# Reciprocal on packed data, variance and response at other places, and one more VectorE tap in four halves

## The reference

```
hdn  = layernorm(mean(x) @ w_fc1.T);  dyn_w = hdn @ w_fc2.T      # a 5x5 kernel for each image and channel
out  = depthwise_conv5x5(x, dyn_w)
out  = layernorm over channels(out) * ln2_w + ln2_b              # per pixel: mean and variance over 64 channels
out  = gelu(out @ w_expand.T)                                    # 64 -> 256 channels
gx   = sqrt(sum over pixels(out^2));  nx = gx / (mean over channels(gx) + eps)
out  = gamma * out * nx + beta + out
out  = out @ w_shrink.T + x                                      # 256 -> 64 channels
```

## Time and profile before

| | us |
|---|---|
| median of three runs | 827.21 |
| profiled execution, time | 827.7 |
| profiled execution, span | 826.0 |
| PE busy | 776.0 (94%) |
| DVE (VectorE) busy | 624.6 (76%) |
| ACT (ScalarE) busy | 398.9 (48%) |
| POOL (GpSimd) busy | 450.2 (55%) |
| chain that ended last, by engine | DVE 17%, PE 11%, ACT 6%, issue 4% |
| mean granted clock of TensorE, as a share of full | 0.982 |

### The profile page before, as it was taken

The page is one execution under the profiler, slowest core; times in us unless marked ns, Lnnn a source line. Parts: engine busy times, 40 slices in busy tenths (PEclk is TensorE's granted clock), DMA queues, the critical chain, the costliest instruction groups (busy, mean ns, idle before and its releaser), DMA issues. The chain is left out here.

```text
span 826.0 us, 15628 instructions
## 1 busy us (share of the span) xinstructions
PE 776.0 (94%) x5399; PEld 635.3 (77%) x5399; DVE 624.6 (76%) x1143; ACT 398.9 (48%) x491; POOL 450.2 (55%) x450
## 2 busy tenths in 40 slices
PE   5999999999999999999999997978899999999886
PEld 5999998999998999999999996644445445454332
DVE  3666666666665666666888887999999999999965
ACT  5591002777774000000000003459989999999981
POOL 2333333333333333335888884988978887888610
PEclk9999999999999999999999996889999999999999
DMA  6670000000000000000000002022233334433234
GB/s 145 162 179 0 0 0 0 2 0 0 0 0 1 1 0 0 0 0 1 1 0 0 0 0 50 25 64 72 77 81 80 90 92 109 104 79 83 55 77 102
DMA packets 61571, 35.81 MB, mean 43 GB/s; under 512 B 41504, under 2 KB 59488, under 8 KB 61536
## 3 DMA queue, kind: packets, MB, share of 16 engines
q1 hardware_dynamic: 59424, 34.83, 17.8%
q10 hardware_dynamic: 2112, 0.52, 0.3%
HBM read 17.85 MB, written 9.37 MB: 33 GB/s over the span
## 5 line engine op out<-in xcount | busy, mean ns | idle before, releaser
L504 PE MATMUL psum<-line_hi,taps_hi 128*128 128x256 f32 x1270 | 203.0, 292 | 11.8 <-DVE taps_lo L400 8.5
L518 PE MATMUL psum<-line_lo,taps_hi 128*128 128x256 f32 x1270 | 202.5, 291 | 0.8 <-DVE line_lo L453 0.8
L512 PE MATMUL psum<-line_hi,taps_lo 128*128 128x256 f32 x1270 | 202.2, 291 | 0.0
L453 DVE SCALAR_TENSOR_TENSOR line_lo<-psum,rest 128x256 fp32r<-128x256 f32 x254 | 108.0, 425 | 123.9 <-POOL rest L285 114.9
L504 PEld LDWEIGHTS psum<-line_hi,taps_hi 128*128 128x128 f32 x1270 | 177.1, 192 | 13.0 <-issue 9.3
L518 PEld LDWEIGHTS psum<-line_lo,taps_hi 128*128 128x128 f32 x1270 | 176.4, 191 | 1.9 <-DVE line_lo L453 1.7
L512 PEld LDWEIGHTS psum<-line_hi,taps_lo 128*128 128x128 f32 x1270 | 176.9, 191 | 0.0
L285 POOL TENSOR_TENSOR rest<-x,line_hi 128x256 f32<-128x256 f32 x127 | 82.9, 652 | 168.6 <-DVE line_hi L444 168.6
L337 ACT ACTIVATE by_h<-x (+1 forms) x128 | 85.7, 669 | 106.6 <-DVE x L433 105.0
L285 POOL TENSOR_TENSOR rest<-by_h,line_hi 128x256 f32<-128x256 f32 x127 | 91.5, 720 | 83.3 <-DVE line_hi L444 83.3
L793 POOL TENSOR_TENSOR part<-part,prod 128x1008 f32<-128x1008 f32 (+2 forms) x56 | 127.5, 2276 | 17.1 <-ACT prod L860 11.3
(11 more groups left out here) (159 smaller groups left out, 760.6 us busy)
## 6 DMA issues: line engine op xcount, KB each, us to landing
stage<-in_x_dram SPq DMA_DIRECT2D x32, 256.0 KB, 4.0
rstd_wide<-rstd_dram SPq DMA_DIRECT2D x30, 256.0 KB, 5.3
out_dram<-x SPq DMA_DIRECT2D x28, 256.0 KB, 5.4
crossed<-x SPq DMA_DIRECT2D x16, 256.0 KB, 3.5
crossed<-x SPq DMA_DIRECT2D x16, 240.0 KB, 3.6
rstd_dram<-rstd SPq DMA_DIRECT2D x15, 64.0 KB, 1.5
out_dram<-x ACTq DMA_DIRECT2D x4, 128.0 KB, 4.7
out_dram<-x SPq DMA_DIRECT2D x4, 128.0 KB, 4.0
```

The costliest lines, as they stand in the source:

```text
L453: dve.scalar_tensor_tensor(out=line_lo[:, (slot + 1) % SLOTS, :, part], in0=as_lines(line_ps[slot][:, 0:LINE]), scalar=0.0, in1=as_lines(r ...
L504: mm = pe.matmul(line_ps[slot][:, 0:LINE], taps_hi[:, s, d, :], line_hi[:, slot, :, d:d + WP], start=(d == 0), stop=(d == OFFSETS - 1))
L512: pe.matmul(line_ps[slot][:, 0:LINE], taps_lo[:, s, d, :], line_hi[:, slot, :, d:d + WP], start=False, stop=False, skip_group_check=True)
L518: mm = pe.matmul(line_ps[slot][:, 0:LINE], taps_hi[:, s, d, :], line_lo[:, slot, :, d:d + WP], start=False, stop=(d == OFFSETS - 1), skip_ ...
```

## The change

- `EARLY` goes from halves 3, 4, 5, 6, 8, 10, 12, 14 to all of 3 to 14: halves 7, 9, 11 and 13 too have eleven VectorE taps and four products.
- The reciprocal of halves 0 to 14 works on packed data. SP copies the 16 partitions of `std` that hold data (four copies, each of 4x128 values) into `dense`, 128 partitions by 16 columns; VectorE waits for all four and takes the reciprocal of `dense`; the store to DRAM is 8 KB and not 64 KB. The spreading copies are of the same size as before.
- In slots without an energy sum `make_var` comes after three taps and not four. `make_rstd` comes after two more taps and after `finish(v,1)`; it was one tap after `make_var`.
- TensorE's `respond` comes ahead of `conv(3)` and not behind it.

```
-EARLY, EARLY_TAP = (3, 4, 5, 6, 8, 10, 12, 14,), ("up", 3)
+EARLY, EARLY_TAP = (3, 4, 5, 6, 7, 8, 9, 10, 11, 12, 13, 14,), ("up", 3)
...
+        PER = UCOLS // C
+        dense = sb("dense", [P, PER])
+        dense_rstd = sb("dense_rstd", [P, 2, PER])
...
-        rstd_dram = nc.dram_tensor("rstd_dram", [2, P, STAT_COLS], F32, kind="Internal").ap()
+        rstd_dram = nc.dram_tensor("rstd_dram", [2, P, PER], F32, kind="Internal").ap()
...
             def spread_rstd(u):
+                sp.wait_ge(std_ready, u + 1)
+                if u > 0:
+                    sp.wait_ge(rstd_ready, u)
+                for g in range(4):
+                    sp.dma_start(dense[32 * g:32 * g + 32, :],
+                                 std[32 * g:32 * g + 2 * SUBS, :].rearrange("q (a n) -> q a n", n=PER)).then_inc(std_dense, 16)
                 sp.wait_ge(rstd_ready, u + 1)
...
-                sp.dma_start(rstd_dram[u % 2], rstd[:, u % 2, :]).then_inc(rstd_stored[u % 2], 16)
+                sp.dma_start(rstd_dram[u % 2], dense_rstd[:, u % 2, :]).then_inc(rstd_stored[u % 2], 16)
...
-                rows = rstd_dram[u % 2].rearrange("(g q) n -> g (q n)", g=4)
+                rows = rstd_dram[u % 2].rearrange("(g h q) n -> g h (q n)", g=4, h=2)
...
-                    mine = rows[:, SUBS * h * STAT_COLS:SUBS * (h + 1) * STAT_COLS].rearrange("(a g) n -> a g n", a=1)
+                    mine = rows[:, h, :].rearrange("(a g) n -> a g n", a=1)
...
             def make_rstd(u):
-                dve.wait_ge(std_ready, u + 1)
                 if u > 1:
                     dve.wait_ge(rstd_stored[u % 2], 16 * (u // 2))
-                dve.reciprocal(rstd[:, u % 2, :], std[:, :]).then_inc(rstd_ready, 1)
+                if u < LAST:
+                    dve.wait_ge(std_dense, 64 * (u + 1))
+                    dve.reciprocal(dense_rstd[:, u % 2, :], dense[:, :]).then_inc(rstd_ready, 1)
+                else:
+                    dve.wait_ge(std_ready, u + 1)
+                    dve.reciprocal(rstd[:, u % 2, :], std[:, :]).then_inc(rstd_ready, 1)
...
                 take(2)
                 if v >= 0:
                     finish(v, 0)
-                take(2)
                 if n in range(UNITS) and n % 2 == 1:
+                    take(2)
                     sum_energy(n // 2)
+                else:
+                    take(1)
                 if w in range(UNITS):
                     make_var(w)
-                take(1)
+                take(2)
+                if v >= 0:
+                    finish(v, 1)
                 if w in range(UNITS):
                     make_rstd(w)
-                take(1)
-                if v >= 0:
-                    finish(v, 1)
                 take(1 + len(dve_taps(s)) - len(DVE_TAPS))
...
                 at_e(0, 1)
-                conv(3)
                 if n in range(UNITS) and n % 2 == 1:
                     respond(n // 2)
+                conv(3)
                 at_e(1, 0)
```

More of the change, by code:

```diff
@@ L655, in block_two @@
         rstd_spread = sem("rstd_spread")
+        std_dense = sem("std_dense")
         spread_made = sem("spread_made")
```

## The result

The changed kernel takes 846.94 us (median of four runs, 845.33 to 847.35) against 827.17 us: the ratio is 1.0233, 95% interval 1.022 to 1.0246, 19.8 us slower. Forecast was 829.2 us in a range of 823 to 837, so the size is far off. The profiled execution is the fastest of the four: 845.33 us with a span of 843.6 us, 17.6 us above the span of before.

What follows compares the result with a forecast made beforehand. VectorE's own order was taken as the bound. First four slots +2.79, halves 5 and 6 -0.21, four pairs -0.32, half 15 -0.24 gave +2.0 us; 827.7 + 2.0 - 0.5 = 829.2 us, range 823 to 837.

Steps and rivals of the forecast that it cites:

- The engine: Block two: VectorE, where the sum must be made, has no idle time to give; an 11/11 pair is 35.76 us.
- The taps and the response: Halves 7, 9, 11, 13 gain a tap; the earlier response removes a 0.8 us wait; pairs go from 35.63 to 35.76.
- The floor of 35.76: Pair of halves with 11 and 11 taps: pure VectorE work without a gap, 35.76 us.
- The packed reciprocal: VectorE, 15 halves before the last: 16 columns take 0.26 us, 0.27 between neighbours, saving about 0.60 us a half.
- The cover: VectorE work hiding the copies: ready at T+3.56 in odd halves, T+3.29 in even ones, T being the variance's start.
- L: Time from first issue of the four packed copies to the last landing, taken as 2.85 us; no change at 2.72.
- far ends: Outer bounds for the time from the copies' first issue to last landing: 2.2 and 5.3 us.
- near ones: Closer bounds for that time: 2.5 (0.33 a step) and 3.1 us (0.53 a step), both with a landing of 1.5.
- The first four slots: Slots 1 to 4, without finish: +1.02, +1.48, +0.41 and +0.68, less 0.80 for the response wait, sum +2.8 us.
- Costs taken as nothing: Later rstd (1.5 us in even halves, 0.3 in odd) hidden by GpSimd's wait for TensorE; SP's queue; the unchanged end.
- Rival 2: SP issues the copies slowly, 0.63 us a step: 8.3 us more, 837.4 us; chance 0.24.
- Rival 3: TensorE still sends the response late, held by ScalarE's gelu: 0.8 us waits stay in five pairs, +4, 833 us; chance 0.05.

Runs made afterwards that it cites:

- e10: Kernel before with eleven taps in all halves from 3 to 14 and nothing else of the change; 828.87 us, ratio 1.0008.
- e11: Kernel before with TensorE's response ahead of conv(3) and nothing else of the change; 823.85 us, ratio 0.9948.
- e3: Changed kernel with a single packed copy, not four, from half 1 on (output isn't the reference's); 826.47 us, ratio 0.9988.
- e4: Changed kernel with its reciprocal two taps later on VectorE, all four copies kept; 825.38 us, ratio 0.9971.
- e8: Changed kernel, packed reciprocal only from half 4 on and two taps later; halves 0 to 3 keep the old reciprocal and order; 822.87 us.
- e1: Changed kernel without packing: 128x128 reciprocal on std in its new place, copies left out, old store and spread; 832.30 us, ratio 1.0072.
- e9: As e8, but with ten taps in halves 7, 9, 11, 13 as in the kernel before; 821.28 us, ratio 0.9917.
- e6: Changed kernel with each copy writing 4 rows of 512 bytes, not 32 of 64, to a scratch tile; 842.05 us, ratio 1.0175.
- e7: Changed kernel with a half's statistics gathered in 16 neighbouring partitions, so that one copy of 128 rows packs them; 858.24 us, ratio 1.0359.
- e5: Changed kernel with two of the four packed copies issued by ScalarE behind its root, two by SP; 844.08 us, ratio 1.0195.

## Why the prediction was wrong

- **The engine.** Right. VectorE's own order is the bound in the pairs: 35.76 for 11/11 (e10), 0.9 us off when the wait for the response goes (e11), 34.6 without any wait (e3, e4, e8). In the first slots it is not VectorE alone (e3, e4).
- **The taps and the response.** The floor of 35.76 was right. What the prediction didn't say is that the two parts compete: the taps fill the time which the response's new place sets free. Each alone is harmless or a gain. Together, with the new places, a pair takes 36.03 us (e1); the two without the new places weren't run.
- **The packed reciprocal.** 0.25 us measured, 0.26 taken. What it costs in VectorE's order was 0.27 in the forecast and is 0.17: the next tap starts at 685.64, 0.17 us behind 685.47. So a half saves 0.69 and not 0.60 us. e1 and e3 agree: their pairs differ by 36.03 - 34.64 = 1.39 us, two reciprocals.
- **The cover.** T+3.56 and T+3.29 were forecast. In e3, where the reciprocal of these slots doesn't wait, it starts at 675.98 - 672.34 = T+3.64 in slot 9 and at 694.04 - 690.53 = T+3.51 in slot 10. The difference is the gap between neighbouring taps of e1, taken too small because the taps in the earlier trace rows had other work between them. It makes the cover longer and the work longer at once, so it doesn't help.
- **L: the step that failed.** "I take 2.85" should have been 4.06. Of the 1.2 us, 0.8 is the spacing of the issues (0.71 measured against 0.45) and 0.4 the landing (1.91 against 1.5), both from e3. The 0.45 a step lay between the lone store of 0.33 us and the small loads at the start, 0.53 on average; the landing was the store's. That store has no issue ahead of it, and it still holds SP for 0.32 us here. Nearer rows were in the trace and weren't used: `crossed`, the only copy within SBUF, holds SP for 0.51 and 0.60 us, and in block two SP issues two by two. SP in slot 9 of the kernel before, behind the store:

```profile
676.68 1.28 SPq L756 DMA_DIRECT2D rstd_wide<-rstd_dram  x2
678.01 1.35 SPq L742 DMA_DIRECT2D out_dram<-x  x2
```

That is 0.64 and 0.67 us an issue. With 0.67 a step and the landing of 1.5 the sum would have been 3.5 and 839 us, still short, since the landing too was too small. The measured L lies within the far ends of the prediction, 2.2 and 5.3; the range of 823 to 837 went with the near ones, and so it was too short. The Trainium skill's fixed cost of about 2.0 us (DMA: Bandwidth & Descriptors, "Anatomy of one DMA") agrees with the 1.91 us of one copy here, although it was read off another way of issuing. It was put aside because of the store.
- **The first four slots.** Forecast +2.8 us at L = 2.85, so 7.6 at 4.06. Measured at half 4: 599.43 - 594.37 = 5.1 us, and 5.8 when the earlier start of block two (528.80 against 529.52) is taken off. Slot 1 costs 1.4 and not 2.2 us: counted from the start of block two, the variance begins 0.7 us sooner than the forecast took (4.37 against 5.09 us). Slot 3 costs 0.9 and not 1.6: there 0.5 us of waits for TensorE and ScalarE are gone that the kernel before had. Slots 2 and 4 came within 0.4 and 0.1 us.
- **Costs taken as nothing.** GpSimd now waits for the factors (68.9 us in 13 waits) in place of TensorE, and no engine waits for GpSimd in the pairs: that cover held. It had help that the prediction didn't count: the copies that spread the packed factors land after 4.0 us and not 5.3 (medians); in e9, which has both forms, 5.3 for the halves with the old one and 4.1 for the packed ones. The end was not free: it loses 1.1 us. TensorE there, in the changed kernel:

```profile
805.79 3.59 PE L1327 MATMUL psum<-wide,shrink_now 128*64 128x512 f32 x8 [4.67 <-DVE x L1104]
```

and its stretch (the last columns are the granted clock, the DMA share and GB/s):

```profile
805.70:809.30 3.60, 3.50 (x8) 0.77 (x8) 1.24 (x3) 2.37 (x3) 1.95 (x1) 0.53 0.11 25
```

TensorE idles 4.67 us for VectorE, is then granted 0.53 of its clock, that is nearly all of the time 1.2 and not 2.4 GHz, and the eight matmuls take 3.59 us against 1.94 us in the kernel before, where the idle time ahead of them was 0.94 us. The last mean square is late by that: VectorE's wait for it is 3.8 us against 2.7. That the copies cause this isn't shown. e10, without any packing, loses the same (its wait is 3.9 us), and e1 idles 3.70 us at this place and then takes 1.94 us and waits 2.7. TensorE in e10:

```profile
789.29 3.63 PE L1312 MATMUL psum<-wide,shrink_now 128*64 128x512 f32 x8 [2.44 <-DVE x L1090]
```

Rival 2 of the prediction (slow issues, 837 us) came nearest, with the right place and too small a price. Rival 3 is out: the response's wait went.

In all, by the trace, in a pair (8 to 10): waits for the copies 1.41 + 1.52 = 2.93 us; two shorter reciprocals -1.38; the waits for the response and the shrink -0.81 and -0.18; the tap +1.3; the lost gaps +0.27. That sums to 2.1 us, and 2.12 was measured. Over the block: up to half 4 +5.06, halves 5 and 6 +1.97, four pairs +8.52, half 15 +0.95, the end +1.12, in all 17.62 us against 17.6 us between the two spans.

What stays open: why a packed copy holds SP for 0.7 us when the store of the factors takes 0.32, and why the landing is longer. That one side lies in DRAM isn't enough, for the stores of the output hold SP for 0.67 each. e6 only shows that the number of rows is the smaller part.

## What to carry to other kernels

A wait in an engine's own order costs its full length as soon as that engine is the bound, so a DMA that feeds such an engine must be priced at issues plus landing, with the spacing read from issues that stand one behind another in the same stretch and not from a lone one, before what it saves is counted. Count the instructions: four small copies cost four issues. When a trace shows that more work on an engine costs nothing, look for the wait that hides it, and take the wait away by itself first: here one moved line (e11) gave 4.3 us, and the packed reciprocal, once it was given enough cover and kept out of the first slots and without the four taps (e9), 2.6 us more.

## What the runs showed of the hardware

- A copy of 2 KB within SBUF takes 1.91 us from its issue to the instruction that waits for it, and the next issue on SP stands 0.71 us behind it (0.64 with rows of 512 bytes, e6). Alone it holds SP for 0.72 to 0.73 us (e3), one of 128 rows for 0.59 (e7), a store of 8 KB to DRAM for 0.32.
- 32 small matmuls (128x128, f32) that go to four groups of 32 columns take 1.1 us; the same to one group take 3.7 us (e7), both at a granted clock of 1.00.
- Two issues on ScalarE's queue keep ScalarE from its next instruction for 1.36 to 1.47 us in every slot but the first, where it is 2.0 (e5).
- A tap of VectorE that waits on a semaphore for the tap before it starts 1.28 us after it, an instruction without that wait 1.17 us after it. With `finish` and the reciprocal as neighbours, and so one such gap a slot unused, a pair takes 0.27 us more (e1 against e10).
- How long TensorE idles doesn't by itself tell the clock that it is granted next. The same eight shrink matmuls near the end take 1.94 us behind 3.70 us of idle time (e1), 3.6 us behind 2.44 (e10, granted clock 0.54), and 2.36, 3.07 and 3.45 us behind 2.46 (e8, e4, e9).
